# A gated attention and expert layer: a second buffer for the stacked queries and a new table of work pieces

## The reference

```python
x = x + jnp.tanh(g_xattn[0]) * attention(_layernorm(x), ctx_512, Wq, w_kc_q, w_kc_kv, W_qr, W_kr, Wo)
x = x + jnp.tanh(g_ffn[0]) * experts(_layernorm(x), router_weight, router_bias, expert_bias)

# attention: 4 batches, 256 rows, 16 heads
q_hk = (hidden_q @ Wq.T).reshape(Bv, Sv, H, K)
q_big = jnp.einsum('bshk,hkq->bshq', q_hk, w_kc_q)
q_big = _apply_rope(q_big, sin_q, cos_q)
kv_r = _apply_rope(kv_c, sin_k, cos_k)
q_r = jnp.einsum('bshq,hqr->bhsr', q_big, W_qr)
k_r = jnp.einsum('bld,hdr->bhlr', kv_r, W_kr)
attn = jax.nn.softmax(jnp.einsum('bhsr,bhlr->bhsl', q_r, k_r), axis=-1)
ctx_c = jnp.einsum('bhsl,bld->bhsd', attn, kv_r)
ctx_lat = jnp.einsum('bhsd,hkd->bhsk', ctx_c, w_kc_kv)
return ctx_lat.transpose(0, 2, 1, 3).reshape(Bv, Sv, H * K) @ Wo.T

# experts: 64 experts, the best 8 of each row
scores = softmax(flat @ router_weight.T + router_bias)
topk_w, topk_idx = jax.lax.top_k(scores, TOP_K)
out = flat * jnp.sum(topk_w, axis=-1, keepdims=True) + jnp.einsum('tk,tkh->th', topk_w, expert_bias[topk_idx])
```

## Time and profile before

| | us |
|---|---|
| median of 3 runs | 297.4 |
| lowest and highest of them | 296.53, 298.22 |
| the profiled execution | 298.57 |
| its span in the trace | 296.8 |

### The profile page before, as it was taken

The page is one execution under the profiler, slowest core; times in us unless marked ns, Lnnn a source line. Parts: engine busy times, 40 slices in busy tenths (PEclk is TensorE's granted clock), DMA queues, the critical chain, the costliest instruction groups (busy, mean ns, idle before and its releaser), DMA issues.

```text
span 296.8 us, 5365 instructions
## 1 busy us (share of the span) xinstructions
PE 273.3 (92%) x1848; PEld 200.5 (68%) x1848; DVE 194.7 (66%) x454; ACT 149.3 (50%) x447; POOL 135.1 (46%) x210
## 2 busy tenths in 40 slices
PE   7996699999999899999998999899989997899786
PEld 7873477567865778487756785678558755668563
DVE  2648888567746676467637764778458736676764
ACT  2401555476446546564457454852473647765332
POOL 2829128603862384235823555237615752433103
PEclk9999899999999999999999999999999999999965
DMA  7995021036000000170000000000000000001012
GB/s 227 259 281 155 1 55 37 1 115 178 2 0 2 0 0 4 44 218 33 2 0 0 2 1 2 0 2 1 2 0 1 3 0 0 2 0 35 4 35 71
DMA packets 15628, 13.19 MB, mean 44 GB/s; under 512 B 5426, under 2 KB 14834, under 8 KB 15474
## 3 DMA queue, kind: packets, MB, share of 16 engines
q1 hardware_dynamic: 15074, 12.46, 15.1%
q10 hardware_dynamic: 528, 0.39, 0.4%
HBM read 11.80 MB, written 1.05 MB: 43 GB/s over the span
## 4 chain that ended last, share of the span: by engine, by line
PE 70%; DVE 11%; ACT 5%; POOL 4%; DMA 3%; issue 3%; SPq 3%; ACTq 0%; POOLq 0%; DVEq 0%
PE ring L910 20%; PE context L1036 8%; PE probs_t L1024 8%; PE scores L1013 6%; PE ring L953 6%; PE ring L936 5%; DVE q_stack L672 5%; PE ring L924 4%; PE scores L1014 4%; DMA rope_q_sb<-in_rope_q 3%; PE ring L875 3%; PE ring L990 2%; ACT q_stack L593 2%; POOL roped L472 2%; ACT probs L602 2%
## 5 line engine op out<-in xcount | busy, mean ns | idle before, releaser
L506 POOL TENSOR_SCALAR probs<-probs,inv_sum 128x256 f32<-128x256 f32 x128 | 59.6, 478 | 96.6 <-DVE inv_sum L818 96.6
L472 POOL TENSOR_TENSOR roped<-roped,cross 128x512 f32<-128x512 f32 x48 | 60.5, 1284 | 32.5 <-DVE cross L686 32.2
L602 ACT ACTIVATE probs<-scores,neg_max 128x256 f32<-128x256 f32 x128 | 59.9, 477 | 11.6 <-DVE neg_max L812 11.3
L612 ACT COPY probs_t_sb<-probs_t 128x512 f32<-128x512 f32 x64 | 37.8, 590 | 53.5 <-PE probs_t L1024 53.3
L812 DVE TENSOR_REDUCE neg_max<-scores 128x2 f32<-128x512 f32 x64 | 43.3, 678 | 7.7 <-PE scores L1014 7.7
L1013 PE MATMUL scores<-keys_hi,q_stack 128*128 128x256 f32 x128 | 39.3, 328 | 7.5 <-DVE q_stack L672 5.0
L685 DVE TENSOR_TENSOR roped<-ring,rope_q_sb 128x512 f32<-128x512 f32 x48 | 33.0, 687 | 15.2 <-PE ring L910 9.9
L1013 PEld LDWEIGHTS scores<-keys_hi,q_stack 128*128 128x128 f32 x128 | 24.6, 192 | 25.6 <-issue 15.8
L1024 PE MATMUL probs_t<-ident,probs 128*128 128x128 f32 x256 | 39.1, 275 | 1.6 <-POOL probs L506 1.3
L910 PE MATMUL ring<-xn_hi,a_hi 128*128 128x512 f32 x96 | 39.3, 409 | 0.3 <-DVE a_lo L672 0.2
L910 PE MATMUL ring<-xn_hi,a_lo 128*128 128x512 f32 x96 | 37.7, 393 | 0.0
(11 more groups left out here) (94 smaller groups left out, 450.6 us busy)
## 6 DMA issues: line engine op xcount, KB each, us to landing
wq_sb<-in_wq SPq DMA_DIRECT2D x4, 512.0 KB, 4.6
wo_t_sb<-in_wo_t SPq DMA_DIRECT2D x4, 512.0 KB, 4.3
w_qr_sb<-in_w_qr SPq DMA_DIRECT2D x4, 384.0 KB, 4.4
w_kc_q_sb<-in_w_kc_q SPq DMA_DIRECT2D x3, 384.0 KB, 4.6
x_sb<-in_x SPq DMA_DIRECT2D x4, 256.0 KB, 7.2
rope_q_sb<-in_rope_q SPq DMA_DIRECT2D x2, 512.0 KB, 7.8
out<-x_sb SPq DMA_DIRECT2D x3, 256.0 KB, 2.2
w_kr_sb<-in_w_kr SPq DMA_DIRECT2D x4, 128.0 KB, 4.3
```

The costliest lines, as they stand in the source:

```text
L472: last = nc.gpsimd.tensor_tensor(roped[:, j, k, :], roped[:, j, k, :], cross[:, done % 2, j, :], ALU.add)
L506: last = nc.gpsimd.tensor_scalar(e, e, inv_sum[:, i % 4, half:half + 1], 1.0, ALU.mult, ALU.mult)
L602: last = nc.scalar.activation(probs[:, i % E_BUFS, half, :], scores[:, i % 2, half, :], ACT.Exp, bias=neg_max[:, i % 4, half:half + 1], ac ...
L612: nc.scalar.copy(probs_t_sb[:, i % T_BUFS], probs_t[:]).then_inc(probs_t_ready, 1)
```

## The change

`q_stack` gets a second buffer, chosen by the parity of the step, so ACT's copies of step n wait for the last scores of step n - 2, no longer of n - 1. The waits of `project` are written for any order of the `a` and `x` pieces, and the scores of steps 0 and 1 now wait for their keys, since the piece `("k", 1)` may now come later.

The functions that made the table are gone; tables written out stand in their place. No piece is added or dropped.

```diff
-        q_stack = sb("q_stack", [P, GH, SPAN], F32R)
+        q_stack = sb("q_stack", [P, 2, GH, SPAN], F32R)
...
-                    if n:
-
-                        act.wait_ge(scores_ready, last_item(n - 1, pair=pair) + 1)
-                    nc.scalar.copy(q_stack[0:64, 2 * pair, :], bank(u - 1 + pair)[0:64, :])
-                    last = nc.scalar.copy(q_stack[64:128, 2 * pair + 1, :], bank(u - 1 + pair)[64:128, :])
+                    if n >= 2:
+
+                        act.wait_ge(scores_ready, last_item(n - 2, pair=pair) + 1)
+                    nc.scalar.copy(q_stack[0:64, n % 2, 2 * pair, :], bank(u - 1 + pair)[0:64, :])
+                    last = nc.scalar.copy(q_stack[64:128, n % 2, 2 * pair + 1, :], bank(u - 1 + pair)[64:128, :])
...
-                pe.wait_ge(ring_free, freed_by[("a", g, GH - 1)])
-                pe.wait_ge(ring_free, freed_by[("x", t, 1)])
+                pe.wait_ge(ring_free, max(freed_by[("a", g, i)] for i in range(GH)))
+                pe.wait_ge(ring_free, max(freed_by[("x", t, dc)] for dc in range(2)))
...
                 pe.wait_ge(ring_free, freed_by[("p", n)] - 1 + head // 2)
+                if n < 2:
+                    pe.wait_ge(ring_free, freed_by[("k", n)])
...
-                    q = q_stack[:, head, b * S + half * P:b * S + (half + 1) * P]
+                    q = q_stack[:, n % 2, head, b * S + half * P:b * S + (half + 1) * P]
...
+STEP_SLOTS = (
...
+        ([("r", 7), ("p", 7)], []),
+        ([], [("out", 5, 6, 2)]),
```

More of the change, by code:

```diff
@@ L56 @@
 SPLIT = ("x", "k", "a", "o", "p")
-def weights(g):
-    return [("a", g, hh) for hh in range(GH)] + [("m", g, 0), ("o", g, 0)]
-def queries(n):
-    return [("q", n, k, j) for k in range(PC) for j in range(2)]
 def pieces_before():
-    w, q = weights(0), queries(0)
-    return [("n", 0), ("n", 1), w[0], ("x", 0, 0), w[1], w[2], ("c",), ("x", 0, 1), w[3], w[4], q[0], q[1],
-            q[2], q[3], q[4], q[5], ("k", 0), ("k", 1), ("n", 2), ("r", 0), ("n", 3), ("p", 0),
-            ("x", 1, 0), ("x", 1, 1), ("a", 1, 0)]
+    return [("n", 0), ("n", 1), ("a", 0, 0), ("a", 0, 2), ("a", 0, 1), ("x", 0, 1), ("x", 0, 0), ("a", 0, 3),
+            ("q", 0, 0, 0), ("c",), ("q", 0, 0, 1), ("q", 0, 1, 0), ("m", 0, 0), ("q", 0, 1, 1), ("q", 0, 2, 0),
+            ("q", 0, 2, 1), ("k", 0), ("n", 2), ("r", 0), ("n", 3), ("p", 0), ("a", 1, 1), ("x", 1, 0), ("x", 1, 1)]
@@ L146, in pieces_after @@
-def pieces_after():
-    return [("out", STEPS - 1, 6, 1), ("out", STEPS - 1, 7, 1), ("turn", 4, 2), ("part", 2, 2),
-            ("pick", 2, 2), ("logit", 4, 2), ("norm", 6, 1), ("norm", 7, 1), ("mix", 2, 2), ("take", 4, 2),
-            ("turn", 6, 1), ("turn", 7, 1), ("logit", 6, 1), ("logit", 7, 1), ("take", 6, 1),
-            ("pick", 4, 2), ("part", 4, 2), ("take", 7, 1), ("pick", 6, 1), ("part", 6, 1), ("part", 7, 1),
-            ("mix", 4, 2), ("pick", 7, 1), ("mix", 6, 1), ("mix", 7, 1)]
+    return [("o", 0, 0), ("q", 1, 0, 0), ("a", 1, 0)]
@@ new lines, in pieces_of_step @@
+def pieces_of_step(n):
+    return STEP_SLOTS[n]
+def pieces_after():
+    return [("turn", 4, 2), ("part", 2, 2), ("out", 7, 6, 1), ("out", 7, 7, 1), ("pick", 2, 2), ("logit", 4, 2),
+            ("norm", 6, 1), ("norm", 7, 1), ("mix", 2, 2), ("turn", 6, 1), ("turn", 7, 1), ("take", 4, 2),
+            ("logit", 6, 1), ("part", 4, 2), ("pick", 4, 2), ("take", 6, 1), ("logit", 7, 1), ("pick", 6, 1),
+            ("part", 6, 1), ("take", 7, 1), ("part", 7, 1), ("mix", 4, 2), ("mix", 6, 1), ("pick", 7, 1),
+            ("mix", 7, 1)]
@@ L804, in pieces @@
                             b = bank(u - 1 + pair)
-                            low(q_stack[64:128, h0, :], b[0:64, :], q_stack[0:64, h0, :], piece, pair)
-                            low(q_stack[0:64, h1, :], b[64:128, :], q_stack[64:128, h1, :], piece, pair
+                            q = q_stack[:, piece[1] % 2]
+                            low(q[64:128, h0, :], b[0:64, :], q[0:64, h0, :], piece, pair)
+                            low(q[0:64, h1, :], b[64:128, :], q[64:128, h1, :], piece, pair
                                 ).then_inc(ring_free, 1)
```

132 lines of the change are left out of this document (71 added, 61 removed), and 8 rows, old and new, of the table STEP_SLOTS.

## The result

| | before | after |
|---|---|---|
| median, us | 297.15 (4 runs) | 287.28 (4 runs) |
| lowest and highest | 296.53, 298.22 | 286.37, 288.11 |
| the profiled execution | 298.57 | 288.11 |
| its span | 296.8 | 286.3 |

The ratio is 0.9649 with a 95% interval of 0.9595 to 0.9703. The forecast was 290.7 us in a range from 287.0 to 295.3: the direction is right, but the gain of 9.9 us is half as large again as the forecast one of 6.7.

What follows compares the result with a forecast made beforehand. PE was taken to bound the kernel, its work fixed and only 8.4 us of middle waits open. Waits gone 7.7, less new waits 2.9, plus tail 1.9, net 6.7 off 297.4: 290.7 us, range 287.0 to 295.3.

Steps and rivals of the forecast that it cites:

- Waits gone, 7.7: PE's middle waits that go: 4.3 us for q_stack, 0.3 ring bank, 2.3 exponentials, 0.8 POOL.
- New waits, 2.9: Waits the new order adds: 0.3 in step 5, 0.5 in step 4, 1.0 in step 6, 0.7 rank product, 0.4 accident.
- 0.3 of exponentials in step 5: Two VectorE rotary products come ahead of the reduction the exponentials need, putting about 0.3 us back.
- 0.5 in step 4: Low part of o waits behind seven ACT instructions, the last item's reciprocal behind it: new wait of 0.5 us.
- starving rank product in steps 1 and 3: With r and p together, p waits for POOL's last sum: 0 to 0.35 us each, taken as 0.7 together.
- queue accident: One more wait for turned probabilities from POOL, like one seen in the old profile: 0.4 us.
- Head, 0: Before the first scores: k1's turns become 0.65 us of bound work, merged weight moves 0.65 into idle time; sum 0.
- Tail, 1.9: Behind the last context: earlier norms, some 0.9 us, and one mix product fewer behind the last pick, 1.0; together 1.9 earlier.
- rival 1: Head: less idle time might hold PE's clock at 2.4 GHz, saving about 1.8 us, giving 288.9; chance 0.10.
- rival 2: Seven steps: waits only move, each step getting back 0.6 us, so 4.2 of 6.7 go, giving 294.9; chance 0.18.
- rival 3: Five steps with r and p together: POOL's sum queues, p comes 2.5 us late, giving 302.5; chance 0.07.
- Rival 4: Whole kernel: PE's work bounds with waits as mere slack, or tables undo each other; time stays 297; chance 0.08.

Runs made afterwards that it cites:

- the piece between p and the scores: The kernel before, with step 6's out piece moved from slot 4 to slot 6, behind p: 297.30 us, ratio 0.9965.
- the lead of the query pieces: The changed kernel, with the first query piece of steps 2, 4 and 6 back in slot 0 of the step: 289.65 us, ratio 0.9715.
- the second profile: The changed kernel run once more with nothing altered: 286.65 us, ratio 0.9626, span 284.9.
- the equal-clock pair: Profiles of the kernel before and of the changed kernel run again, with the same half clock at start and end: spans 296.8 and 284.9 us.

## Why the prediction was wrong, and where it was right

The direction and the main mechanism were right: the forecast waits went. The gain came out half as large again because three terms failed: the new waits (2.9 forecast, 0.91 measured), what a wait and a split of the rank product cost beyond the idle time, which the sum put at nothing (2.36), and step 0, put at 0 with the head (up to step 1 the gain is 1.8 at an equal clock). The tail was too large in the other direction.

**Waits gone, 7.7.** Right. In steps 1 to 6 of before the brackets are those of the earlier trace rows, and in the changed kernel only two are left, both forecast. The wait of scores for `q_stack` was forecast to fall from 5.0 to 0.7 and did. The single experiments show two of the mechanisms apart: the piece between p and the scores, and the lead of the query pieces.

**New waits, 2.9.** This step failed, by 2. The wait on ACT's copy in step 6 is there with 0.91 for 1.0. None of the others is: no 0.3 of exponentials in step 5, no 0.5 in step 4, no starving rank product in steps 1 and 3 (0.7; no line of r or p waiting in a step), no queue accident (0.4). For the rank product I took the far end of 0 to 0.35 each on the ground that VectorE is busy two thirds of the time; the near end was right. Both bounds stood in the prediction; the choice between them was the mistake. In step 1 the last query piece ends at 84.87 and POOL's sum at 88.79, 3.92 us later where I had 4.2 to 4.8, and p begins 0.37 behind it; in step 3 both figures are the same:

```profile
86.28 2.51 POOL L486 TENSOR_TENSOR roped<-roped,cross 128x512 f32<-128x512 f32 x2 [2.90 <-DVE cross L700]
89.16 0.59 PE L951 MATMUL ring<-roped,m_sb 64*64 64x512 f32 x1
```

**What no row of waits shows, 2.36.** This term was missing. I took PE's work as fixed and only its idle time as movable. The split of the rank products shows 0.3 in each of two steps, 0.9 with the third. The rest is the price of a wait beyond its bracket, since idle time is counted from the modelled end of a pipelined matmul. The timelines show it when the distance between two matmuls' starts, less the bracket, is set beside the same pair of pieces where nothing waits. Scores behind a turn start 0.03 us after its last matmul without a wait and 0.27 plus the bracket with one: 0.24 lost, for a bracket of 0.78 as for one of 2.11. Scores behind an out piece lose 0.16, a turn behind scores 0.16, scores behind a merged `o` 0.07. Over the eleven waits of steps 1 to 6 before this is 1.91 us, over the two after 0.32, so 1.6 less. With the 0.9 that makes 2.5 for 2.36. The 1.6 was read from the traces of both kernels; no experiment took it apart from the waits. The Trainium skill ("Perfetto Trace Analysis", Identifying the Most-Contended Engine) warns that matmul busy time is a bad metric since matmuls are pipelined; the trace agrees in that 3.8 us of the gain lie in busy time at an equal count of matmuls.

**Head, 0.** Right for the head as far as the runs can tell, wrong for what I left out behind it. The kernel with the old head reaches step 1 no later. That k1 costs some 0.65 in step 0 was right in kind (0.48, 0.40). But step 0 lost more than its bracket of 0.25 from the new slots, 0.7 with equal pieces, and the whole stretch up to step 1 came 1.8 sooner at an equal clock, of which a part is scatter of the head (first scores between 34.33 and 35.38 in eleven profiles with the new head, two of them with k1 in it, and between 35.15 and 35.95 in four with the old). In the first profile the longer half clock hid all of it, and the term looked right by accident.

**Tail, 1.9.** Right in sign, too large: 1.16 at an equal clock, 1.57 in the profiled pair. I had all of it behind the last context and put the logits moved behind the last turn at 0, between 0.7 gained and 0.6 lost. Both happened: a wait of 0.68 ahead of the last context is gone and it comes 0.8 sooner, counted from step 7's first scores (27.41 for 28.20), and the output piece behind it 0.9 later than it could. So of the 1.16 only 0.37 was won behind the last context. The norms come 7.03 us behind it instead of 7.18, 0.15 sooner and not 0.9, as the additions start 0.9 later. And the last pick starts 15.65 behind it in both kernels at an equal clock; that only one mix product follows it saves 0.37 and not 1.0, since that product now waits 0.44 for ACT's copy. The forecast that the last VectorE addition starts 1.5 to 2 us sooner behind the last context is wrong: 18.11 us before, 17.36 after, 17.74 in the second profile.

**Sum.** Against 6.7: two more for waits that didn't come, 2.4 for what no wait shows, 1.8 for head and step 0, 0.7 less for the tail; that gives 12.2, less 0.25 of the ring's wait in step 0 that is counted twice, 11.9, as the equal-clock pair shows. The medians show 9.9 in the first comparison and 11.4 in the last one.

**Rivals.** The clock in the head, rival 1, was not held by `("a", 1, 1)`: with the very same order it fell for 3.4 or 6.8 us. In two profiles out of eleven with this move it held, in none of four with the old head; that is too few to say whether the move helps. But that the clock there is worth a bound of its own was right. Waits that only move, rival 2, is what the single pieces show (1.0 of 1.4 given back in steps 6 and 7, more than all in step 1) and the whole table does not. The rank product did not starve, rival 3: L951's wait is the 0.7 of the head. Rival 4 fell with the result, and its first half was wrong in an instructive way: the waits weren't slack, they cost more than they showed.

## What to carry to other kernels

A second buffer is worth nothing while nobody waits for the first to come free: look which queue the producer stands in before adding one. To shorten a chain through several engines, put independent pieces between its ends, but price each at the place that it leaves, for it was covering something there. And when two orders have the same work in a stretch, compare the stretch's length by the starts of one landmark instruction: it repeats to 0.03 us, takes in what the idle figures hide, and lets a part of 0.3 us be seen in a kernel whose whole time scatters by 1 to 2.

## What the runs showed of the hardware

- Half clock at the start came for 0, 3.4 or 6.8 us, and began anywhere from 26 to 36 us, in kernels with the same order up to there, and in the same kernel (6.8 and 3.4). Where it began at 26 to 27 us, it came with PE's wait of 2.1 us for VectorE ahead of the rank product; where it began at 33 to 36, with the waits of 1.4 to 2.1 us for the turned inputs. Two kernels with the same waits had none. 3.4 us of it in a step cost 0.8 us (28.95 for 28.17), less than half of 3.4, as the faster one waits 0.68 us for VectorE in this step and the slower one doesn't. The Trainium skill ("TensorE: Matmul & The Clock Gate", What's actually happening) has the slow clock as the default that activity lifts. The runs agree in that it always fell within or behind idle time, and show that one order of instructions can land on either side.
- In one kernel it fell in the middle, behind a single wait of 2.20 us, and took 1.6 us more: that wait cost nearly twice its length.
- At the end PE runs at half clock for 4.2 to 11.2 us, by the execution, and the stretch from step 7's first scores to PE's end is 43.6 us with 4.2 of it and 45.1 with 9.9, with the same order.
- Splitting a rank product, so that PE went once more from 128 by 128 to 64 by 64 products and back, cost 0.3 us a time, with no wait to show it; some 0.2 of it is seen at entry and exit.
- A wait of PE cost 0.07 to 0.24 us more than the idle time in its bracket, by what stands on its two sides, and the same for 0.78 us of idle time as for 2.11.
